# Two chained attention blocks on one core: the stacked queries of the second block loaded through ScalarE's DMA queue

## Chip, cores, metric

One Trainium2 chip, one core. The metric is the device time of one launch of the whole kernel, in microseconds (us).

## What is computed

64 independent sequences of 128 rows and 320 channels go through two blocks. Cut to what matters here:

```python
# first block (8 heads of 40): cross attention on the context, plus a small attention of four context tokens
query = x @ Wq;  keyt = enc @ Wk;  valt = enc @ Wv
hs = mha(query, keyt, valt)
x = (hs + token_attention(...)) @ Wout + b_out + x
# second block (20 heads of 16)
h1 = ln(x);  x = attn(h1, h1, q1, k1, v1, o1_w, o1_b, 20) + x     # self attention
h2 = ln(x);  x = attn(h2, context, q2, k2, v2, o2_w, o2_b, 20) + x  # cross attention
h3 = ln(x);  a, g = split(h3 @ ff_w1 + ff_b1);  x = (a * gelu(g)) @ ff_w2 + ff_b2 + x
```

The change touches the queries and keys of the second block's self attention (`h1 @ q1` and `h1 @ k1`).

## The kernel before

The 64 sequences are taken two at a time, so the loop has 32 steps and one more that drains what is still under way: it runs 33 times. The work is software-pipelined by hand. One pass of the loop holds the self attention of one pair of sequences, the first block of the next pair, and the feed-forward of an earlier one. Each engine has its own instruction stream, and within a stream all is in program order; the streams meet only at semaphores. The order is written out by hand: the table `BODY` gives the order of TensorE's outputs ("jobs"), which go round six PSUM banks, and each engine's loop lists its calls.

Scores run in units of four heads. `ALL_UNITS` numbers them: units 0 to 3 are the token attention (tile names `ca_heads`, `G`, values `VX`), 4 to 13 the self attention, 14 to 23 the cross attention (both `Qs`, `Ks`), 24 to 27 the first block (`Q0s`, `K0s`). For a unit n, `scores(i, n)` on TensorE gives the row maxima that VectorE takes, `exponents(i, n)` computes the transposed scores less the maxima, ScalarE's `exps(i, n)` writes the exponentials twice (L724 in 32 bits to `P`, L725 in 16 bits to `PT`), GpSimd's `low_probabilities(i, n)` (L501) writes the 16-bit remainder, and TensorE's `attend(i, n)` waits for that remainder (`low_p`) before it multiplies by the values.

Queries and keys are kept as a 16-bit high part and a 16-bit remainder. ScalarE writes the high part (`cQ`, `cK`, L653), VectorE the 32-bit whole, GpSimd the remainder (L508), and then they make a round trip through DRAM to be laid out by head. A **put** (`put_split`, L359) stores one of three chunks to a scratch tensor (`s_k1`, `s_q1`); a **stack** (`stack`, L363) reads a scratch tensor back by three loads of 160 KB, so that high and low parts lie in stacked partitions of `Ks` and `Qs`. All of these transfers are issued by SyncE, in the order of `one_pass` (L413 to L438). For the self attention that order is: the puts of Q0T (first-block queries), K1T and Q1T, three each; `stack_self`, which waits until all six puts of K1T and Q1T have landed (`self_put` at 96) and then issues the three loads of `Ks` and the three of `Qs`; `stack_first_queries` (three loads of `Q0s`); then the puts of K0T, the first of which waits until all six stack loads have landed (`self_stacked`).

TensorE's scores of unit 4 wait for the same six loads. `self_put` has two more readers: ScalarE's `emptied` waits for it before it overwrites `cK` (K0T) and `cQ` (Q2T).

ScalarE's stretch around the change is in its loop: three `high_shifted` of K1T, three of Q1T, `high_maxima(i, 0)` (L695), `exps(i, 0)`, `exps(i, 1)`, `high_maxima(i, 1)`, and then the first-block values and `exps(i, 2)`. It issues no DMA.

Of the kernel before, what the change touches and what calls it, by code (L numbers as in the profile page):

```python
# [14 lines left out]
D0, D1 = H // HEADS0, H // HEADS1  # L15
# [32 lines left out]
Q_PARTS = (0, 0, 1)  # L48
# [32 lines left out]
SPLITS = {"K1T": 0, "Q1T": 3, "Q2T": 6}  # L81
SPLITS_STEP = 9
LOADS_STEP = 16 * 9
STACK_LOADS, STACK_STORES = 16 * 6, 16 * 6
CROSS_STORES = 16 * 3
WAIT_BASE = 16 * 6
HEAD_LINKS, STEP_LINKS = 30, 27
# [69 lines left out]
LOOP_JOBS = Jobs(BODY)  # L157
# [24 lines left out]
def build(nc, d, out):  # L182
# [4 lines left out]
    with ctx:  # L187
# [3 lines left out]
        def sem(name):  # L191
            return ctx.enter_context(nc.semaphore(name))
# [109 lines left out]
        j_full, a_done, v_done = sem("j_full"), sem("a_done"), sem("v_done")  # L302
        low_p, pv_done, o_done = sem("low_p"), sem("pv_done"), sem("o_done")
        split_done = sem("split_done")
        self_put, q0_put, k0_put = sem("self_put"), sem("q0_put"), sem("k0_put")
        q2_put, k2_put = sem("q2_put"), sem("k2_put")
        self_stacked, first_stacked, cross_stacked = sem("self_stacked"), sem("first_stacked"), sem("cross_stacked")
        vx_ready, ca_ready = sem("vx_ready"), sem("ca_ready")
# [9 lines left out]
        def done(i, number, who):  # L318

            return (i + 1) * PER[who] + number + 1  # L320
# [26 lines left out]
        def _(sp):  # L347
# [13 lines left out]
            def stack(dst, src, e, parts, landed):  # L361
                for y, part in enumerate(parts):
                    sp.dma_start(dst[y * e:(y + 1) * e, :, :],  # L363
                                 src[part, :, :].rearrange("(h e) n -> e h n", e=e)).then_inc(landed, 16)
# [17 lines left out]

            def stack_self(i):
                sp.wait_ge(j_full, done(i - 1, LOOP_JOBS.number("T23"), "J"))
                sp.wait_ge(self_put, i * STACK_STORES + STACK_STORES)
                stack(Ks, s_k1, D1, K_PARTS, self_stacked)
                stack(Qs, s_q1, D1, Q_PARTS, self_stacked)

            def stack_first_queries(i):
                sp.wait_ge(j_full, done(i - 1, LOOP_JOBS.number("T27"), "J"))  # L390
# [23 lines left out]
            def one_pass(i, stores):  # L414
                put_low(i, "Q0T", 0, cQ, CH0, s_q0, AT0, q0_put)
                put_low(i, "Q0T", 1, cQ, CH0, s_q0, AT0, q0_put)
                put_low(i, "Q0T", 2, cQ, CH0, s_q0, AT0, q0_put)
                put_split(i, "K1T", 0, cK, s_k1, self_put)
                put_split(i, "K1T", 1, cK, s_k1, self_put)
                put_split(i, "K1T", 2, cK, s_k1, self_put)  # L420
                put_split(i, "Q1T", 0, cQ, s_q1, self_put)
                put_split(i, "Q1T", 1, cQ, s_q1, self_put)
                put_split(i, "Q1T", 2, cQ, s_q1, self_put)
                stack_self(i)
                stack_first_queries(i)
                put_low(i, "K0T", 0, cK, CH0, s_k0, AT0, k0_put, self_stacked)
                put_low(i, "K0T", 1, cK, CH0, s_k0, AT0, k0_put)
                load_next(i)
                put_low(i, "K0T", 2, cK, CH0, s_k0, AT0, k0_put)
                stack_first_keys(i)  # L430
                stack_cross_keys(i)
                put_split(i, "Q2T", 0, cQ, s_q2, q2_put, first_stacked)
                put_split(i, "Q2T", 1, cQ, s_q2, q2_put)
                put_split(i, "Q2T", 2, cQ, s_q2, q2_put)
                stack_cross_queries(i)
                put_low(i, "K2T", 0, cK, CH1, s_k2, AT1, k2_put, cross_stacked)
                put_out(i, 0, stores)
                put_out(i, 1, stores)  # L438
                put_low(i, "K2T", 1, cK, CH1, s_k2, AT1, k2_put)
                put_low(i, "K2T", 2, cK, CH1, s_k2, AT1, k2_put)  # L440
# [189 lines left out]
        def _(act):  # L630
# [9 lines left out]
            def emptied(i, name):  # L640

                return {"Q0T": (q2_put, i * CROSS_STORES + CROSS_STORES), "K1T": (k2_put, i * CROSS_STORES + CROSS_STORES),
                        "Q1T": (q0_put, i * CROSS_STORES + CROSS_STORES), "K0T": (self_put, i * STACK_STORES + STACK_STORES),
                        "Q2T": (self_put, i * STACK_STORES + STACK_STORES),
                        "K2T": (k0_put, i * CROSS_STORES + CROSS_STORES)}[name]

            def high_shifted(i, name, k, dst, c):
# [9 lines left out]
            def high_chunk(i, name, k, dst, r, f):  # L657

                bank = bank_of(i, LOOP_JOBS, f"{name}{k}")
                if k == 0:  # L660
                    act.wait_ge(factor_ready, i + 1)
                    act.wait_ge(*emptied(i, name))
                nc.scalar.activation(dst[0:r, 0, k, :], bank[0:r, 0:GS], ACT.Copy,
                                     scale=factor[0:r, f:f + 1]).then_inc(a_done, 1)

            def high_tokens(i, jobs):

# [81 lines left out]
            with nc.Fori(0, STEPS + 1, engines=[act.engine], hint_back_edge=True) as i:  # L749
                L = LOOP_JOBS  # L750
                order.restart()
                high_chunk(i, "Q0T", 0, cQ, CH0[0], FQ0)
                high_chunk(i, "Q0T", 1, cQ, CH0[1], FQ0)
                high_blocks(i, "XT0_0", hTn, 0)
                high_blocks(i, "XT0_1", hTn, 1)
                high_chunk(i, "Q0T", 2, cQ, CH0[2], FQ0)
                high_shifted(i, "K1T", 0, cK, 0)
                high_shifted(i, "K1T", 1, cK, 0)
                high_shifted(i, "K1T", 2, cK, 0)
                high_shifted(i, "Q1T", 0, cQ, 3)  # L760
                high_shifted(i, "Q1T", 1, cQ, 3)
                high_shifted(i, "Q1T", 2, cQ, 3)
                high_maxima(i, 0)
                exps(i, 0)
                exps(i, 1)
                high_maxima(i, 1)
                first_part(i, "V0", 0, V0, HEADS0, D0, factor[:, F0:F0 + 1])
                exps(i, 2)
                high_chunk(i, "K0T", 0, cK, CH0[0], FK0)
                first_part(i, "V1", 0, V1, HEADS1, D1, V1_FACTOR)  # L770
                exps(i, 3)
                high_chunk(i, "K0T", 1, cK, CH0[1], FK0)
                high_chunk(i, "K0T", 2, cK, CH0[2], FK0)
                first_part(i, "V1", 1, V1, HEADS1, D1, V1_FACTOR)
                first_part(i, "V0", 1, V0, HEADS0, D0, factor[:, F0:F0 + 1])
                high_maxima(i, 2)
                exps(i, 4)
                exps(i, 5)
                exps(i, 6)
                high_maxima(i, 3)  # L780
                exps(i, 7)
                exps(i, 8)
                exps(i, 9)
                exps(i, 10)
                exps(i, 11)
                exps(i, 12)
                exps(i, 13)
                gelu(i, L, 0)
                high_out(i, 1, 0)
                gelu(i, L, 1)  # L790
                gelu(i, L, 2)
                gelu(i, L, 3)
                high_out(i, 1, 1)
                gelu(i, L, 4)
                gelu(i, L, 5)
                high_blocks(i, "XT1_0", hTn, 0)
                high_blocks(i, "XT1_1", hTn, 1)
                high_shifted(i, "Q2T", 0, cQ, 6)
                high_shifted(i, "Q2T", 1, cQ, 6)
                high_shifted(i, "Q2T", 2, cQ, 6)  # L800
                gelu(i, L, 6)
                gelu(i, L, 7)
                gelu(i, L, 8)
                gelu(i, L, 9)
                exp4(i)
                load_exp_table()
                high_maxima(i, 4)
                high_chunk(i, "K2T", 0, cK, CH1[0], FK2)
                exps(i, 14)
                exps(i, 15)  # L810
                high_chunk(i, "K2T", 1, cK, CH1[1], FK2)
                exps(i, 16)
                high_maxima(i, 5)
                exps(i, 17)
                high_chunk(i, "K2T", 2, cK, CH1[2], FK2)
                exps(i, 18)
                exps(i, 19)
                exps(i, 20)
                exps(i, 21)
                high_maxima(i, 6)  # L820
                exps(i, 22)
                exps(i, 23)
                high_out(i, 2, 0)
                high_maxima(i, 7)
                exps(i, 24)
                exps(i, 25)
                exps(i, 26)
                exps(i, 27)
                high_out(i, 2, 1)
                first_part(i, "V2", 0, V2, HEADS1, D1, factor[:, F2:F2 + 1])  # L830
                high_out(i, 0, 0)
                first_part(i, "V2", 1, V2, HEADS1, D1, factor[:, F2:F2 + 1])
                high_out(i, 0, 1)
                high_blocks(i, "XT2_0", hT3, 0)
                high_blocks(i, "XT2_1", hT3, 1)
                high_tokens(i, L)
                assert order.next == PER["A"]
# [1072 lines left out]
```

## Time and profile before

| | us |
|---|---|
| median of 3 runs | 4137.58 |
| the three runs | 4137.58, 4140.25, 4123.45 |
| the profiled execution, device time | 4125.89 |
| its span, first to last instruction | 4124.0 |
| TensorE busy in it | 3767.4 (91%) |
| ScalarE busy in it | 2225.3 (54%) |
| VectorE, GpSimd busy in it | 2501.0 (61%), 1981.5 (48%) |

The profile is of one execution; the device time lies 1.9 us over its span. In its lists a wait stands with the group of instructions that waited and with what ended the wait; "L363" is a line of the kernel; names of tiles stand as written<-read, and buffer numbers are left out. DMA issues stand on the queue of the engine that issues them (SPq is SyncE's), with the time that the issue took; the landing is told apart. PEclk is the granted clock of TensorE as a share of full speed, 1.00 at 2.4 GHz and 0.50 at 1.2 GHz.

### The profile page before, as it was taken

Reading aid. Unit: us, or ns where it says so; the run is one execution under the profiler, and the core shown is the slowest. Engines: PE = TensorE matmul, PEld = TensorE weight load, DVE = VectorE, ACT = ScalarE, POOL = GpSimd, SP = SyncE. Lnnn points to the kernel's source line nnn. Section 1 sums busy time; section 2 is a strip of 40 time slices with the busy share of each in tenths; the row PEclk is TensorE's granted clock in tenths of the full one; section 3 lists DMA queues with packets and bytes.
Section 4 is the critical chain, followed back from the end, with each engine's and each line's share of the span. In section 5 each row is a group of like instructions: output and inputs, shape, how many; then the busy total and the mean of one; then the engine's idle time right before and its main releaser. Section 6 shows DMA issues by size and latency. Waiting matters only on the chain.

```text
span 4124.0 us, 114798 instructions
## 1 busy us (share of the span) xinstructions
PE 3767.4 (91%) x39220; PEld 3033.2 (74%) x39220; DVE 2501.0 (61%) x6482; ACT 2225.3 (54%) x3834; POOL 1981.5 (48%) x2297
## 2 busy tenths in 40 slices
PE   4899999999999999999999999999999999999999
PEld 4677777777777777777777777777777777777777
DVE  7565655566566556656655565665556566555655
ACT  1465555545545554655555455555555555555554
POOL 0445454544544554454455445445445544554453
PEclk9899999999999998999999899999989999998999
DMA  4323222333322333332233323223332322333230
GB/s 137 57 55 58 47 46 49 62 59 57 62 42 46 55 61 60 57 62 42 47 54 58 62 56 63 43 47 54 59 62 56 61 45 49 52 58 62 56 64 19
DMA packets 393942, 230.78 MB, mean 56 GB/s; under 512 B 24807, under 2 KB 393055, under 8 KB 393183
## 3 DMA queue, kind: packets, MB, share of 16 engines
q1 hardware_dynamic: 393566, 224.70, 28.9%
q8 instruction: 366, 6.00, 0.7%
q14 instruction: 10, 0.07, 0.0%
HBM read 148.59 MB, written 76.02 MB: 54 GB/s over the span
## 4 chain that ended last, share of the span: by engine, by line
issue 42%; POOL 41%; PE 11%; DVE 4%; POOLq 2%; ACT 0%; DMA 0%; DVEq 0%; SPq 0%; ACTq 0%
POOL PT L501 24%; PE bank L1377 11%; POOL ca_heads L542 3%; POOL rstd L550 2%; POOL XB L478 2%; POOL cK L508 2%; POOL cQ L508 2%; POOL VX L526 1%; POOL OA L525 1%; POOL XA L478 1%; POOL rstd L549 1%; POOL X L478 1%; POOLq L500 1%; POOL ca L541 1%; POOL ca L539 0%
## 5 line engine op out<-in xcount | busy, mean ns | idle before, releaser
L501 POOL TENSOR_TENSOR PT<-P,PT 128x512 f16<-128x512 f32 (+1 forms) x924 | 1069.2, 1157 | 778.3 <-ACT PT L725 778.3
L976 DVE TENSOR_REDUCE mx<-bank 128x4 f32<-128x512 f32 (+1 forms) x924 | 582.7, 680 | 107.9 <-PE bank L1377 103.9
L1377 PE MATMUL bank<-hT,w_ff_w 128*128 128x256 f16 x5440 | 644.4, 273 | 1.7 <-DVE hT L1005 1.5
L1377 PEld LDWEIGHTS bank<-hT,w_ff_w 128*128 128x128 f16 x5440 | 523.3, 98 | 74.8 <-issue 7.9
L1377 PE MATMUL bank<-mxs,pick 84*128 84x128 f16 (+1 forms) x3696 | 543.7, 229 | 0.0
L1377 PEld LDWEIGHTS bank<-mxs,pick 84*128 84x128 f16 (+1 forms) x3696 | 394.2, 109 | 25.9 <-issue 14.5
L1377 PE MATMUL bank<-Qs,Ks 96*128 96x128 f16 x2640 | 382.3, 228 | 27.4 <-DVE mxs L985 27.0
L1377 PE MATMUL bank<-w_ff,F 128*128 128x320 f32 x1360 | 401.5, 438 | 1.3 <-DVE F L1052 1.3
L706 ACT ACTIVATE P<-bank,ff_b,scale 128x256 f32<-128x256 f32 x340 | 192.0, 565 | 370.2 <-PE bank L1377 271.4
L1377 PEld LDWEIGHTS bank<-V,PT 128*128 128x128 f16 (+1 forms) x9504 | 313.6, 96 | 76.4 <-POOL PT L501 51.3
L1377 PE MATMUL bank<-V,PT 128*128 128x17 f16 (+1 forms) x9504 | 346.5, 173 | 17.2 <-POOL PT L501 12.6
L1023 DVE RECIPROCAL rden<-bank 128x20 f32<-128x20 f32 (+1 forms) x264 | 64.0, 242 | 481.5 <-PE bank L1377 480.5
L1377 PEld LDWEIGHTS bank<-w_ff,F 128*128 128x128 f32 x1360 | 245.3, 190 | 83.2 <-DVE F L1052 1.5
L1377 PEld LDWEIGHTS bank<-Qs,Ks 96*128 96x128 f16 x2640 | 266.2, 102 | 54.5 <-DVE mxs L985 34.5
L724 ACT ACTIVATE P<-bank,log_p,exp_self 128x512 f32<-128x512 f32 x330 | 255.2, 773 | 76.9 <-PE bank L1377 76.7
L724 ACT ACTIVATE P<-bank,log_p,out_factor 128x512 f32<-128x512 f32 x330 | 254.6, 771 | 75.5 <-PE bank L1377 68.4
L508 POOL TENSOR_TENSOR cQ<-whole,cQ 128x256 f16<-128x256 f32 (+1 forms) x198 | 132.2, 668 | 312.1 <-DVE whole L869 312.1
L869 DVE TENSOR_SCALAR whole<-bank,factor,qk_b 128x256 f32<-128x256 f32 (+1 forms) x297 | 160.8, 541 | 186.9 <-ACT cQ L653 156.0
L549 POOL TENSOR_TENSOR rstd<-mv,eps 128x1 f32<-128x1 f32 x198 | 41.5, 209 | 455.3 <-DVE mv L1040 455.3
L724 ACT ACTIVATE P<-bank,log_p,factor 124x512 f32<-124x512 f32 (+1 forms) x264 | 205.2, 777 | 100.8 <-PE bank L1377 97.6
L725 ACT ACTIVATE PT<-bank,log_p,out_factor 128x512 f16<-128x512 f32 x330 | 253.3, 768 | 0.0
L725 ACT ACTIVATE PT<-bank,log_p,exp_self 128x512 f16<-128x512 f32 x330 | 253.3, 768 | 0.0
(282 smaller groups left out, 7814.3 us busy)
## 6 DMA issues: line engine op xcount, KB each, us to landing
Ks<-scratch_k SPq DMA_DIRECT2D x198, 160.0 KB, 5.4
Qs<-scratch_q SPq DMA_DIRECT2D x198, 160.0 KB, 5.7
scratch_k<-cK SPq DMA_DIRECT2D x134, 128.0 KB, 1.8
scratch_q<-cQ SPq DMA_DIRECT2D x134, 128.0 KB, 1.8
Q0s<-scratch_q SPq DMA_DIRECT2D x99, 160.0 KB
K0s<-scratch_k SPq DMA_DIRECT2D x99, 160.0 KB
cT<-in_cT SPq DMA_DIRECT2D x136, 96.0 KB, 2.0
xin<-in_x SPq DMA_DIRECT2D x34, 320.0 KB, 3.2
```

The costliest lines, as they stand in the source:

```text
L478: nc.gpsimd.tensor_tensor(dst[:, b, :], src[:, b, :], bias[:, j, :], ALU.add).then_inc(ready, 1)
L501: nc.gpsimd.tensor_tensor(PT[0:keys, n % PT_SLOTS, 1, :], P[0:keys, n % P_SLOTS, :], PT[0:keys, n % PT_SLOTS, 0, :], ALU.subtract).then_in ...
L508: nc.gpsimd.tensor_tensor(dst[0:r, 1, k, :], whole[0:r, m % 3, :], dst[0:r, 0, k, :], ALU.subtract)\
L542: nc.gpsimd.tensor_tensor(ca_heads[:, :, :], ca16[:, :].unsqueeze(1).to_broadcast([rows, HEADS0, GS]), mask_ca[:, :].unsqueeze(2).to_broad ...
L549: link(i, nc.gpsimd.tensor_tensor(rstd[:, j, b:b + 1], mv[:, j, b, 1:2], eps[:, :], ALU.add))
L550: nc.gpsimd.tensor_tensor(rstd[:, j, b:b + 1], rstd[:, j, b:b + 1], minus_half[:, :], ALU.pow)\
L706: nc.scalar.activation(gate[:, t % 2, :], bank[:, 0:GS], ACT.Gelu, scale=scale[:, 1:2], bias=ff_b[:, FFT + t:FFT + t + 1]).then_inc(a_done, 1)
L724: nc.scalar.activation(P[0:keys, n % P_SLOTS, :], bank[0:keys, :], ACT.Exp, bias=log_p[0:keys, :], scale=by)
L725: nc.scalar.activation(PT[0:keys, n % PT_SLOTS, 0, :], bank[0:keys, :], ACT.Exp, bias=log_p[0:keys, :], scale=by).then_inc(a_done, 1)
L869: nc.vector.tensor_scalar(whole[0:r, m % 3, :], bank[0:r, 0:GS], factor[0:r, FQ2:FQ2 + 1], qk_b[0:r, c + k:c + k + 1], ALU.mult, ALU.add). ...
L976: nc.vector.tensor_reduce(mx[:, g % 2, 4 * u:4 * u + 4], bank[:, :].rearrange("p (h s) -> p h s", h=4)[:, :, 0:keys], axis=AX.X, op=ALU.ma ...
L1377: return nc.tensor.matmul(o, lhsT, rhs, start=start, stop=stop)
```

## The change

`self_put`, one semaphore for six puts, becomes `k1_put` and `q1_put`, 48 each. `stack_self` on SyncE waits for the three puts of K1T alone and issues only the three loads of `Ks`. A new `stack_queries` on ScalarE, called between `high_maxima(i, 0)` and `exps(i, 0)`, waits for the three puts of Q1T and issues the three loads of `Qs` from ScalarE's own DMA queue. `emptied` reads `k1_put` for K0T and `q1_put` for Q2T. All six loads still count on `self_stacked`, whose readers are unchanged. Nothing else moves in any stream.

```diff
@@ SyncE
             def stack_self(i):
                 sp.wait_ge(j_full, done(i - 1, LOOP_JOBS.number("T23"), "J"))
-                sp.wait_ge(self_put, i * STACK_STORES + STACK_STORES)
+                sp.wait_ge(k1_put, i * CROSS_STORES + CROSS_STORES)
                 stack(Ks, s_k1, D1, K_PARTS, self_stacked)
-                stack(Qs, s_q1, D1, Q_PARTS, self_stacked)
...
-                put_split(i, "K1T", 0, cK, s_k1, self_put)
+                put_split(i, "K1T", 0, cK, s_k1, k1_put)
...
-                put_split(i, "Q1T", 0, cQ, s_q1, self_put)
+                put_split(i, "Q1T", 0, cQ, s_q1, q1_put)
...
@@ ScalarE
-                        "Q1T": (q0_put, i * CROSS_STORES + CROSS_STORES), "K0T": (self_put, i * STACK_STORES + STACK_STORES),
-                        "Q2T": (self_put, i * STACK_STORES + STACK_STORES),
+                        "Q1T": (q0_put, i * CROSS_STORES + CROSS_STORES), "K0T": (k1_put, i * CROSS_STORES + CROSS_STORES),
+                        "Q2T": (q1_put, i * CROSS_STORES + CROSS_STORES),
...
+            def stack_queries(i):
+
+                act.wait_ge(j_full, done(i - 1, LOOP_JOBS.number("T23"), "J"))
+                act.wait_ge(q1_put, i * CROSS_STORES + CROSS_STORES)
+                for y, part in enumerate(Q_PARTS):
+                    nc.scalar.dma_start(Qs[y * D1:(y + 1) * D1, :, :],
+                                        s_q1[part, :, :].rearrange("(h e) n -> e h n", e=D1)).then_inc(self_stacked, 16)
...
                 high_maxima(i, 0)
+                stack_queries(i)
                 exps(i, 0)
```

## Rows read from the trace of the kernel before

**Rows 1.** The page, part 1 (engines) and part 2 (granted TensorE clock by slice)

```profile
PE 3767.4 (91%) x39220; PEld 3033.2 (74%) x39220; DVE 2501.0 (61%) x6482; ACT 2225.3 (54%) x3834; POOL 1981.5 (48%) x2297
...
PEclk9899999999999998999999899999989999998999
```

**Rows 2.** Waits of TensorE: us in total, times, longest

```profile
PE bank L1377 <- DVE mxs L985: 88.3, 73, 1.9
...
PE bank L1377 <- POOL PT L501: 34.3, 60, 1.0
...
PE bank L1377 <- DMA Qs<-scratch_q: 9.6, 18, 0.8
```

**Rows 3.** TensorE's groups: forms, xcount, busy us, mean ns, idle before by releaser

```profile
L1377 PE MATMUL bank<-Ks,Qs 96*128 96x128 f16 x2640 | 204.1, 227 | 13.8 <-DMA Qs<-scratch_q 9.6 <-ACT PT L725 4.2
...
L1377 PE MATMUL bank<-VX,PT 128*128 128x41 f16 x1584 | 63.5, 184 | 21.7 <-POOL PT L501 21.7
```

**Rows 4.** Whole steps, one window each: length, busy, PEclk, DMA share, GB/s

```profile
128.90:252.90 124.00, 116.11 (x1176) 93.23 (x1176) 72.80 (x191) 66.84 (x116) 59.67 (x70) 0.90 0.27 51
...
3864.70:3981.50 116.80, 107.64 (x1176) 86.85 (x1176) 72.90 (x192) 66.51 (x115) 59.66 (x70) 0.99 0.29 56
...
sum 3852.60, PE 3573.01 PEld 2871.18 DVE 2335.75 ACT 2133.09 POOL 1909.22; mean PE 111.66 PEld 89.72 DVE 72.99 ACT 66.66 POOL 59.66
```

**Rows 5.** 12 us of each step, from 4 us behind the first maxima copy

```profile
132.90:144.90 12.00, 12.00 (x77) 8.17 (x76) 2.85 (x8) 6.39 (x12) 8.36 (x9) 0.63 1.04 129
...
256.90:268.90 12.00, 10.45 (x114) 8.18 (x114) 5.92 (x19) 7.06 (x14) 9.45 (x10) 1.00 1.03 125
```

**Rows 6.** Timeline of one step, SyncE's queue: start, us, tiles, xcount

```profile
2178.11 2.43 SPq L359 DMA_DIRECT2D scratch_q<-cQ  x3
2182.05 1.33 SPq L363 DMA_DIRECT2D Ks<-scratch_k  x3
2183.43 1.46 SPq L363 DMA_DIRECT2D Qs<-scratch_q  x3
2185.07 2.31 SPq L363 DMA_DIRECT2D Q0s<-scratch_q  x3
```

**Rows 7.** The same stretch, ScalarE

```profile
2178.43 0.25 ACT L695 ACTIVATE mxs<-bank 8x128 f16<-8x128 f32 x1
...
2181.28 0.78 ACT L724 ACTIVATE P<-bank,log_p,factor 128x512 f32<-128x512 f32 x1 [2.60 <-PE bank L1377]
...
2183.95 0.25 ACT L695 ACTIVATE mxs<-bank 8x128 f16<-8x128 f32 x1
```

**Rows 8.** The same stretch, GpSimd

```profile
2182.81 1.16 POOL L501 TENSOR_TENSOR PT<-P,PT 128x512 f16<-128x512 f32 x1 [2.88 <-ACT PT L725]
```

**Rows 9.** The same stretch, TensorE: attend of the first unit, second-block scores

```profile
2184.02 0.47 PE L1377 MATMUL bank<-VX,PT 128*128 128x41 f16 x12 [1.04 <-POOL PT L501]
...
2193.48 1.06 PE L1377 MATMUL bank<-Ks,Qs 96*128 96x128 f16 x16 [0.55 <-DMA Qs<-scratch_q]
```

**Rows 10.** The step before it: SyncE, ScalarE, GpSimd, TensorE

```profile
2061.74 1.33 SPq L363 DMA_DIRECT2D Ks<-scratch_k  x3
...
2061.36 0.78 ACT L724 ACTIVATE P<-bank,log_p,factor 128x512 f32<-128x512 f32 x1 [3.00 <-PE bank L1377]
...
2062.88 1.16 POOL L501 TENSOR_TENSOR PT<-P,PT 128x512 f16<-128x512 f32 x1 [3.27 <-ACT PT L725]
...
2064.44 0.63 PE L1377 MATMUL bank<-VX,PT 128*128 128x41 f16 x12
```

**Rows 11.** Tile Qs: durations min/median/max of its loads' issues, and issue to landing

```profile
L363 SPq DMA_DIRECT2D Qs<-scratch_q x198: 326/457/468, 133.7 to 4042.9; - x198
...
DMA to landing us min/median/max: 3.3/5.7/9.4
```

**Rows 12.** Waits of SyncE's queue

```profile
SPq L363 <- DMA scratch_q<-cQ: 86.9, 64, 1.5
```

More of the change, by code:

```diff
@@ L83 @@
 LOADS_STEP = 16 * 9
-STACK_LOADS, STACK_STORES = 16 * 6, 16 * 6
+STACK_LOADS = 16 * 6
 CROSS_STORES = 16 * 3
@@ L304, in build @@
         split_done = sem("split_done")
-        self_put, q0_put, k0_put = sem("self_put"), sem("q0_put"), sem("k0_put")
+        k1_put, q1_put, q0_put, k0_put = sem("k1_put"), sem("q1_put"), sem("q0_put"), sem("k0_put")
         q2_put, k2_put = sem("q2_put"), sem("k2_put")
@@ L417, in one_pass @@
                 put_low(i, "Q0T", 2, cQ, CH0, s_q0, AT0, q0_put)
-                put_split(i, "K1T", 0, cK, s_k1, self_put)
-                put_split(i, "K1T", 1, cK, s_k1, self_put)
-                put_split(i, "K1T", 2, cK, s_k1, self_put)
-                put_split(i, "Q1T", 0, cQ, s_q1, self_put)
-                put_split(i, "Q1T", 1, cQ, s_q1, self_put)
-                put_split(i, "Q1T", 2, cQ, s_q1, self_put)
+                put_split(i, "K1T", 0, cK, s_k1, k1_put)
+                put_split(i, "K1T", 1, cK, s_k1, k1_put)
+                put_split(i, "K1T", 2, cK, s_k1, k1_put)
+                put_split(i, "Q1T", 0, cQ, s_q1, q1_put)
+                put_split(i, "Q1T", 1, cQ, s_q1, q1_put)
+                put_split(i, "Q1T", 2, cQ, s_q1, q1_put)
                 stack_self(i)
```

## Prediction

> **What bounds the kernel now.** I began with the page's engine table. TensorE is busy 91% of the span and the next engine 61% [rows 1], so a delay counts if it reaches TensorE, and a gain counts if TensorE was waiting. The second view is therefore TensorE's list of waits. The loads that the change touches stand in it with 9.6 us in 18 waits, 0.53 us each [rows 2], and the groups show that all of them are in front of the scores of `Qs` and `Ks` [rows 3]. No other DMA that the loop issues stands among TensorE's waits, so 9.6 us of 4126 is all that earlier stacks can give directly. The same list has 34.3 us of waits for the low probabilities `PT` of GpSimd [rows 2], of which 21.7 us in 22 waits are in front of `attend` on `VX`, the token attention [rows 3]. That wait lies just behind the place where ScalarE gets its new work.
>
> The third view is the step as a whole. There are 32 windows from one step to the next, 120.4 us on average (3852.60 / 32). They fall into two kinds: 16 with the granted clock at 0.97 or above, on average 117.8 us, and 16 at 0.90 to 0.94, on average 123.0 us [rows 4] (an early slow one, the last, a quick one, and the sum). TensorE's clock thus makes 5.1 us of difference in a step. In the 12 us behind the place of the change, 18 of 33 windows have a clock of 1.00 and 15 have 0.53 to 0.67 [rows 5] (the first of each kind); 18 is also the number of waits for `Qs`. So in the quick steps TensorE is early and waits half a microsecond for `Qs`; in the slow ones it runs at half clock and `Qs` is there before it.
>
> **The change part by part.** I take one quick step and the slow step before it.
>
> *What ScalarE now does ahead of the exponentials.* It waits for the last put of Q1T to land. In the quick step that is when SyncE now issues the first load of `Ks`, at 2182.05 [rows 6]; it is held by that landing, since SyncE's queue waits at this line for a put of queries, up to 1.5 us [rows 12]. Then ScalarE issues three loads. On SyncE the same three took 1.46 us [rows 6], one 326 to 468 ns [rows 11]. Nothing in the trace shows what an issue costs ScalarE. The bounds are 0 (only the wait is left) and 2.31 us, which three `Q0s` loads took on SyncE with loads queued ahead of them [rows 6]. I take 1.46, because these are the same transfers. The Trainium skill ("Perfetto Trace Analysis", DMA Instruction — HWDGE) says that the issuing sequencer is occupied until the descriptors are generated and only then takes its next instruction; no row here shows it for ScalarE, and by it the value is the same 1.46.
>
> *What is queued behind it.* `exps(0)`, `exps(1)`, `high_maxima(1)`, then the values. `exps(0)` started at 2181.28 [rows 7] and would start at 2182.05 + 1.46 = 2183.5, 2.2 us later (0.8 to 3.1 by the bounds). GpSimd starts the low part 1.53 us behind that (2182.81 [rows 8]), and TensorE's `attend` starts as soon as it is done: at 2184.02, already after 1.04 us of waiting [rows 9]. There is no slack, so `attend` comes 2.2 us later and that wait grows to 3.3 us. `high_maxima(1)` moves from 2183.95 [rows 7] to about 2186.2; the `T2` product that needs it comes after the first-block values and is covered.
>
> *What it costs in a quick step.* From `attend` to the scores of `Qs` TensorE has one stretch of work that ended at 2193.48 − 0.55 = 2192.9, and then it waited 0.55 us for `Qs` [rows 9]. With 2.2 us more ahead of it, it gets there at 2195.2. The 0.5 us of waiting is gone, covered by the new delay, and 1.7 us are left. 18 × 1.7 = 31 us.
>
> *In a slow step.* The put landed at 2061.74 and `exps(0)` had started at 2061.36, so it is delayed by 0.38 + 1.46 = 1.8 us. The low part then ends at 2062.88 + 1.16 + 1.84 = 2065.9, and `attend`, which went at 2064.44 without a wait [rows 10], is late by 1.4. 15 × 1.4 = 21 us.
>
> *The loads.* `Ks` is issued when the last put of Q1T has been issued, 2178.11 + 2.43 = 2180.5, instead of 2182.05; `Qs` at 2182.05 instead of 2183.43; but `Q0s`, which stood behind `Qs`, now goes out at about 2181.9 [rows 6] and shares the engines with it. At worst `Qs` is the last of nine loads of 160 KB: 1475 kB at 125 GB/s, as in the 12 us of a quick step [rows 5], is 11.8 us from 2181, so about 2193. TensorE comes at 2195.2, or at 2193.7 if issuing costs ScalarE nothing. So I cost the new order of loads at nothing; if that cover is gone, it costs the lateness at one for one. The put of K0T, which waits for the six loads, and the first-block stacks can be late without anybody waiting: no wait of TensorE names them [rows 2]. `emptied` now reads earlier counts, and ScalarE comes there later than both: nothing.
>
> *The sum of the waits alone:* 31 + 21 = 52 us.
>
> *The clock.* TensorE's longest wait in the loop is now 1.9 us, in front of `exponents` for the maxima `mxs` [rows 2], and 1.04 us at `attend` come a little behind. With these two, the clock was low near here in 15 of 33 steps. The second now becomes 3.3 us, longer than any wait of the loop. What share of the 18 quick steps then falls to half clock no row tells: between none and all. I take 11, two in three, at the 5.1 us between the two kinds: 11 × 5.1 = 56 us. Bounds 0 and 18 × 5.1 = 92.
>
> Together 52 + 56 = 108 us. Against the profiled execution's 4125.9 that is 4234; the median of the runs is 12 us above that execution, and the three differ by 17, so I take half of it: 4240.
>
> **The rivals.**
> - *Held, but the clock stays as it is.* For it: the waits that precede a fall are there in both kinds of step. Then 4126 + 52 + 6 = 4184.
> - *Issuing costs ScalarE next to nothing.* Only the wait for the put remains: 0.77 us in a quick step, of which the 0.55 at the scores gives back most (18 × 0.22 = 4), and 0.38 in a slow one, up to 15 × 0.4 = 6. 4136, with half the median's offset 4142. For it: a DMA issue isn't counted as busy. The Trainium skill ("DMA: Bandwidth & Descriptors", Issuing engines are not separate DMA queues) calls the saved issue time usually small and says that all issuers share the 16 DMA engines; the share of 1.03 in [rows 5] agrees that these engines are full here, so a second queue brings `Qs` no sooner than bytes allow.
> - *ScalarE is held longer*, because SyncE issues `Q0s` in the same microseconds: 2.31 us for three and the wait, 3.1 in a quick step less 0.5, 2.7 − 0.4 in a slow one: 18 × 2.6 + 15 × 2.3 = 81, and all 18 steps lose their clock, 92: 4126 + 81 + 92 + 6 = 4305.
> - *Faster.* TensorE's 9.6 us for `Qs` goes, because `Ks` starts 1.5 us and `Qs` 1.4 us earlier, and `attend` isn't delayed: 4126 − 10 + 6 = 4122. It needs ScalarE to get past the put before 2181.28. Against it: the put lands at 2182.05 and nothing ahead of it has changed [rows 6, 7].
>
> **How the numbers follow.** Chances: forecast (around 4240) 0.50, held with an unchanged clock 0.20, issue nearly free 0.12, held longer 0.13, faster 0.05. Range 4145 to 4310: it takes in the forecast with 0 to 18 falls and the second bound of the issue, and leaves out the case of a free issue and the faster one. A measurement of this kernel can tell about 0.5% from no change, that is 4117 to 4158: faster 0.05, same 0.12, slower 0.83.
>
> **What the profile after would show.** On ScalarE's queue three loads of `Qs`, each taking some 0.3 to 0.5 us, and `exps(0)` behind the last of them, about 5 us behind the end of the first maxima copy instead of 2.6 to 3.0. TensorE's wait for `PT` at `attend` on `VX` grows from 21.7 us to 18 × 3.3 + 15 × 1.4 = 80 us. The wait for `Qs` at the scores is gone. More than 15 of 33 windows behind that place have a clock under 1.00. The forecast is wrong if ScalarE's issue is far from 0.5 us, if `attend` turns out to have slack, or if the loads land later than 2195 on this scale, so that the wait for `Qs` grows instead.

## The result, and the profile after

The changed kernel takes 4293.6 us (median of four runs, 4293.0 to 4294.0) against 4138.8 for the kernel before (one run more than ahead of the prediction): a ratio of 1.038, 95% interval 1.036 to 1.041. It is slower, by 155 us; the forecast was 4240 with a range of 4145 to 4310. The profiled execution has a span of 4291.5 us, 167.5 more than the one before.

The page of the changed kernel: engines, granted clock by slice, and ScalarE's new DMA queue (q10).

```profile
PE 3851.2 (90%) x39220; PEld 3108.6 (72%) x39220; DVE 2494.4 (58%) x6482; ACT 2223.6 (52%) x3834; POOL 1979.2 (46%) x2297
...
PEclk9999999999999998999999999999999999999999
...
q10 hardware_dynamic: 33264, 16.23, 3.8%
```

Against [rows 1]: the same 39220 matmuls take 3851.2 us instead of 3767.4. So TensorE is busy 83.8 us longer with the same work, which is a lower clock (0.927 granted on average, 0.947 before); the other 83.7 of the 167.5 are idle time. VectorE, ScalarE and GpSimd are busy no longer than before. Where the idle time is, TensorE's waits of the changed kernel tell (us in total, times, longest), and its groups (busy us, mean ns, idle before by releaser):

```profile
PE bank L1385 <- POOL PT L500: 126.0, 68, 3.5
PE bank L1385 <- DVE mxs L993: 85.0, 72, 1.9
```

```profile
L1385 PE MATMUL bank<-Ks,Qs 96*128 96x128 f16 x2640 | 226.5, 242 | 0.5 <-DMA Qs<-scratch_q 0.5
L1385 PE MATMUL bank<-VX,PT 128*128 128x41 f16 x1584 | 62.8, 183 | 113.6 <-POOL PT L500 113.6
```

[Rows 2, 3] had 34.3 us of waits for `PT`, 21.7 of them in front of `attend` on `VX`; now it is 126.0 and 113.6. The wait for `Qs` at the scores of `Ks` fell from 9.6 us to 0.5, and the idle time of that group from 13.8 to 0.5. So the one group gained 13.3 us and the other lost 91.9.

Whole steps of the changed kernel, as in [rows 4]: two neighbours and the sum of the 32.

```profile
2387.40:2513.50 126.10, 114.99 (x1176) 92.56 (x1176) 72.86 (x192) 66.63 (x116) 59.61 (x70) 0.92 0.30 52
2513.50:2637.20 123.70, 112.06 (x1176) 90.06 (x1176) 72.96 (x192) 66.64 (x116) 59.62 (x70) 0.94 0.30 53
...
sum 4013.60, PE 3652.47 PEld 2943.72 DVE 2329.26 ACT 2131.43 POOL 1906.82; mean PE 114.14 PEld 91.99 DVE 72.79 ACT 66.61 POOL 59.59
```

A step takes 125.4 us (4013.60 / 32) instead of 120.4. The quick steps, with a clock of 0.99 and 107.6 us of busy TensorE [rows 4], are gone. The 12 us behind the place of the change show why (as in [rows 5]; 32 of the 33 windows have 0.72 as the second line, one has 0.59):

```profile
1638.30:1650.30 12.00, 9.03 (x52) 6.03 (x52) 2.37 (x6) 6.47 (x11) 7.54 (x8) 0.59 1.04 108
...
2391.40:2403.40 12.00, 8.55 (x49) 5.77 (x49) 2.28 (x6) 6.00 (x11) 7.53 (x8) 0.72 1.02 108
```

No window is at 1.00 any more, where 18 of 33 were. One step in the timeline (start, us, tiles, number; in brackets the idle time before and what ended it), where the first maxima copy ends at 2135.54:

```profile
2135.29 0.25 ACT L702 ACTIVATE mxs<-bank 8x128 f16<-8x128 f32 x1
2137.61 1.44 SPq L363 DMA_DIRECT2D Ks<-scratch_k  x3
2138.95 1.33 ACTq L670 DMA_DIRECT2D Qs<-scratch_q  x3
2139.23 1.16 SPq L363 DMA_DIRECT2D Q0s<-scratch_q  x3
2140.55 0.78 ACT L731 ACTIVATE P<-bank,log_p,factor 128x512 f32<-128x512 f32 x1 [5.01 <-PE bank L1526]
2142.07 1.15 POOL L500 TENSOR_TENSOR PT<-P,PT 128x512 f16<-128x512 f32 x1 [5.29 <-ACT PT L732]
2143.28 0.60 PE L1385 MATMUL bank<-VX,PT 128*128 128x41 f16 x12 [3.45 <-POOL PT L500]
2143.72 2.48 PE L1385 MATMUL bank<-w_Wv,cT 96*128 96x320 f32 x4
...
2155.17 1.06 PE L1385 MATMUL bank<-Ks,Qs 96*128 96x128 f16 x16
```

Read it from the top. The loads of `Qs` are issued from 2138.95 to 2140.28, and `exps(0)`, which stands behind them in ScalarE's stream, starts at 2140.55, 5.01 us behind the maxima copy (2.60 and 3.00 in [rows 7, 10]). The label "<-PE bank" on its idle time misleads: for that bank alone it would have started at 2.60 as in [rows 7]; the profile counts neither the semaphore wait nor the three issues as work. GpSimd follows 1.52 us later, TensorE waits 3.45 us, and the product behind the wait, four matmuls on `cT`, takes 2.48 us. In the quick step of [rows 9], at full clock, it took 1.32:

```profile
2184.33 1.32 PE L1377 MATMUL bank<-w_Wv,cT 96*128 96x320 f32 x4
```

So at the end of that wait the clock drops to half. The scores of `Ks` start 19.6 us behind the maxima copy; in [rows 9] it was 14.8.

### The profile page after: what moved, and what is told of

Its sections match the earlier page's. It is cut to its first block, busy times and chain, and to the rows that moved or that the text cites. A ratio compares the mean times of both kernels' runs of the same rounds, so it can differ in the third digit from the quotient of the medians.

```text
span 4291.5 us, 114831 instructions
## 1 busy us (share of the span) xinstructions
PE 3851.2 (90%) x39220; PEld 3108.6 (72%) x39220; DVE 2494.4 (58%) x6482; ACT 2223.6 (52%) x3834; POOL 1979.2 (46%) x2297
## 4 chain that ended last, share of the span: by engine, by line
issue 43%; POOL 40%; PE 11%; DVE 4%; POOLq 1%; ACT 0%; DMA 0%; DVEq 0%; SPq 0%; ACTq 0%
POOL PT L500 23%; PE bank L1385 10%; POOL ca_heads L541 3%; POOL rstd L549 2%; POOL XB L477 2%; POOL cK L507 2%; POOL cQ L507 2%; POOL XA L477 1%; POOL VX L525 1%; POOL OA L524 1%; POOL rstd L548 1%; POOL X L477 1%; POOLq L499 1%; POOL ca L540 1%; POOL ca L538 0%
## 5 line engine op out<-in xcount | busy, mean ns | idle before, releaser
L1385 PE MATMUL bank<-mxs,pick 84*128 84x128 f16 (+1 forms) x3696 | 562.0, 234 | 0.0
L1385 PEld LDWEIGHTS bank<-mxs,pick 84*128 84x128 f16 (+1 forms) x3696 | 405.5, 112 | 31.7 <-issue 18.3
L1385 PE MATMUL bank<-Qs,Ks 96*128 96x128 f16 x2640 | 401.0, 235 | 24.1 <-DVE mxs L993 23.7
L1385 PEld LDWEIGHTS bank<-Qs,Ks 96*128 96x128 f16 x2640 | 276.4, 106 | 50.2 <-DVE mxs L993 31.2
L1385 PE MATMUL bank<-hTn,w_q 128*128 128x256 f16 (+1 forms) x1584 | 256.9, 331 | 0.0
```

Of the source, the lines that this page charges most:

```text
L1385: return nc.tensor.matmul(o, lhsT, rhs, start=start, stop=stop)
```

## The experiments

Each is timed beside the kernel before on the same chip. The median of that kernel was 4138.8 us beside the changed kernel, 4127.6 beside e1 to e4, 4118.3 beside e5 to e8 and 4116.6 beside e9 to e11, so kernels of different groups are best compared by ratio. "Held" stands for the theory of the forecast: three issues and their wait hold ScalarE, hence `attend`, hence TensorE's clock. The base is told with each; line numbers differ a little between kernels.

**e1: keys early alone** (base: the kernel before). The split semaphores and the early `Ks`, with `Qs` still on SyncE behind a wait of its own; ScalarE issues nothing.

```diff
-                sp.wait_ge(self_put, i * STACK_STORES + STACK_STORES)
+                sp.wait_ge(k1_put, i * CROSS_STORES + CROSS_STORES)
                 stack(Ks, s_k1, D1, K_PARTS, self_stacked)
-                stack(Qs, s_q1, D1, Q_PARTS, self_stacked)
...
+            def stack_self_queries(i):
+                sp.wait_ge(q1_put, i * CROSS_STORES + CROSS_STORES)
+                stack(Qs, s_q1, D1, Q_PARTS, self_stacked)
...
                 stack_self(i)
+                stack_self_queries(i)
```

> The change without its ScalarE part: the semaphores are split and the keys' loads go out as soon as the keys are put, but the queries' loads stay on SyncE's queue, behind a wait for their own puts; ScalarE issues nothing. Theory 'ScalarE is held' (the wait for the puts and the three issues on ScalarE delay the first exponentials, TensorE waits for their low part, and the clock falls behind that wait): back to the time of before, 4110 to 4150, first exponentials 2.6 to 3.0 us behind the first maxima copy, wait for PT in front of attend on VX about 22 us in all, wait for Qs at the scores below the 9.6 us of before, because the loads start 1.4 us earlier. Rival 'loads' (what costs is that keys' loads now go out while the puts land, or that first-block loads share the engines with the queries'): the part of it that the early keys cause stays, 4200 or more.

Measured: 4111.4 us, ratio 0.995 (0.993 to 0.997). `Qs` lands 12.7 us behind the maxima copy (median; 14.6 before), the scores no longer wait for it, and `attend` waits as before:

```profile
L1389 PE MATMUL bank<-Ks,Qs 96*128 96x128 f16 x2640 | 202.7, 226 | 4.8 <-ACT PT L737 4.3
L1389 PE MATMUL bank<-VX,PT 128*128 128x41 f16 x1584 | 63.0, 183 | 26.3 <-POOL PT L505 26.3
```

The half of the change that concerns the keys is a small gain by itself (0.5%), so the loss is in the other half.

**e2: the wait without the issues** (base: e1). ScalarE waits for the puts of Q1T ahead of `exps(0)`, and issues nothing.

```diff
                 high_maxima(i, 0)
+                act.wait_ge(q1_put, i * CROSS_STORES + CROSS_STORES)
                 exps(i, 0)
```

> As e1_keys_early, but ScalarE waits for the queries' puts ahead of the first exponentials, and issues nothing. It parts the wait from the three issues. Theory 'ScalarE is held': first exponentials at 3.4 to 3.5 us behind the first maxima copy (2.6 to 3.0 before, 5.0 after the change), the wait at attend about 1.9 us in a quick step, so 18 x 0.3 + 15 x 0.4 = 11 us of waits, and the clock falls in some more of the 33 steps than the 15 of before: 4140 to 4220. Rival 'the issues are what holds' (the wait is hidden): 4110 to 4150. Rival 'the wait is all': 4280 to 4300.

Measured: 4183.6 us, ratio 1.013 (1.008 to 1.017). In one step:

```profile
1359.88 0.78 ACT L736 ACTIVATE P<-bank,log_p,factor 128x512 f32<-128x512 f32 x1 [3.70 <-DMA scratch_q<-cQ]
...
1362.62 0.47 PE L1390 MATMUL bank<-VX,PT 128*128 128x41 f16 x12 [2.14 <-POOL PT L505]
```

The exponentials start at 3.70, `attend` waits 2.14 us, and the clock falls just behind it in 32 of 33 steps (in e1 and in the kernel before in none). The waits at `attend` come to 70.0 us, 44 more than in e1, where 11 more were expected: all steps but one wait the 2.14 us, those that had been slow too. From e1 to the changed kernel the ratio goes from 0.995 to 1.038, some 180 us; 0.017 of it (72 us) is the wait for the put alone, and the other 0.026 comes with the issues.

**e9: one issue of three** (base: the changed kernel). SyncE issues the first two loads of `Qs`, ScalarE only the third.

```diff
+            def stack_self_queries(i):
+                sp.wait_ge(q1_put, i * CROSS_STORES + CROSS_STORES)
+                stack(Qs, s_q1, D1, Q_PARTS[0:2], self_stacked)
...
+                stack_self_queries(i)
...
                 act.wait_ge(q1_put, i * CROSS_STORES + CROSS_STORES)
-                for y, part in enumerate(Q_PARTS):
+                for y, part in ((2, Q_PARTS[2]),):
```

> Keys early as in the changed kernel, but ScalarE issues only the third load of the queries, ahead of the first exponentials; SyncE issues the other two behind its own wait for the puts of Q1T. ScalarE is held: one issue less than the changed kernel's three leaves about 0.3 to 0.5 us on ScalarE, so the exponentials start about 4.0 us behind the first maxima copy (3.7 with the wait alone, 5.0 with three issues), attend waits about 2.4 us in every step, the clock falls in all 33 steps, and the time is 4190 to 4240, nearer the kernel with the wait alone (4184). Rival, what counts is that a second queue carries query loads at all: near the changed kernel's 4290. Rival, issues cost nothing: 4184, with attend's wait at 2.1.

Measured: 4204.4 us, ratio 1.021 (1.018 to 1.024). One step, with the issue at 309 ns:

```profile
1351.21 0.31 ACTq L675 DMA_DIRECT2D Qs<-scratch_q  x1
...
1351.79 0.78 ACT L736 ACTIVATE P<-bank,log_p,factor 128x512 f32<-128x512 f32 x1 [4.01 <-DMA scratch_q<-cQ]
...
1354.53 0.47 PE L1390 MATMUL bank<-VX,PT 128*128 128x41 f16 x12 [2.44 <-POOL PT L505]
```

Zero, one and three issues give starts of 3.70, 4.01 and 5.02, waits of 2.14, 2.44 and 3.45, and 4184, 4204 and 4294 us (ratios 1.013, 1.021 and 1.038). What ScalarE issues appears one for one at `attend`.

**e8: the landing sooner in the changed kernel** (base: the changed kernel). SyncE holds the first-block stacks back until `Ks` and `Qs` have landed.

```diff
             def stack_first_queries(i):
+                sp.wait_ge(self_stacked, i * STACK_LOADS + STACK_LOADS)
```

> The changed kernel with the same one edit as e7_behind_alone: first-block loads only behind the six self loads. Theory 'ScalarE is held': the queries land sooner than 15.5 us, at 12.5 to 14, and nothing comes of it, because TensorE reaches the scores at 19.8 us: 4280 to 4300, wait at attend on VX about 114 us. Rival 'loads' (the later landing is part of the cost): 4260 or less.

Measured: 4294.0 us, ratio 1.042 (1.039 to 1.045), the time of the changed kernel. `Qs` lands 3.1 us sooner (12.7 instead of 15.8) and nothing is gained:

```profile
L1386 PE MATMUL bank<-Ks,Qs 96*128 96x128 f16 x2640 | 226.1, 242 | 0.0
L1386 PE MATMUL bank<-VX,PT 128*128 128x41 f16 x1584 | 62.7, 183 | 113.1 <-POOL PT L501 113.1
```

The order of the loads costs nothing in the changed kernel, as the forecast had it: `attend` comes too late for it to matter.

**e3 and e7: ScalarE issues later.** e3 is the changed kernel with the three issues behind `high_maxima(1)`; e7 is e3 with e8's wait on SyncE.

```diff
                 high_maxima(i, 0)
-                stack_queries(i)
                 exps(i, 0)
                 exps(i, 1)
                 high_maxima(i, 1)
+                stack_queries(i)
```

> The change with the same three loads on ScalarE's queue, but called behind the first two exponentials and the second maxima copy. Theory 'ScalarE is held': first exponentials again 2.6 to 3.0 us behind the first maxima copy, the wait for PT at attend on VX back at about 22 us; the queries are issued at about 5.6 instead of 3.4 us and land 1 to 2 us later than after the change, so the scores wait for Qs 1 to 3 us in the quick steps, 20 to 50 us in all: 4140 to 4200. Rival 'loads' (a second queue beside SyncE's is what costs): stays at 4270 to 4310.

> e3_loads_behind, where the queries' loads on ScalarE's queue were issued at 4.5 us and landed only at 18 to 19 us, with one edit: SyncE waits for the six self loads before it issues the three first-block loads. Theory 'sharing' (the queries on the second queue are late because the first-block loads run beside them): the queries land at 13 to 14.7 us, the scores wait at most 0.6 us, 4105 to 4150. Rival 'the second queue is slow by itself': they land at 16 us or later, 4200 or more.

Measured: e3 4257.4 us, ratio 1.030 (1.023 to 1.036); e7 4097.8, ratio 0.995 (0.992 to 0.997). The first lines are e3's, the second e7's:

```profile
L1385 PE MATMUL bank<-Ks,Qs 96*128 96x128 f16 x2640 | 238.5, 250 | 100.0 <-DMA Qs<-scratch_q 97.0 <-DVE V L898 2.2 <-ACT PT L732 0.8
L1385 PE MATMUL bank<-VX,PT 128*128 128x41 f16 x1584 | 69.9, 192 | 24.8 <-POOL PT L500 24.8
```

```profile
L1386 PE MATMUL bank<-Ks,Qs 96*128 96x128 f16 x2640 | 200.2, 225 | 5.3 <-ACT PT L733 5.2
L1386 PE MATMUL bank<-VX,PT 128*128 128x41 f16 x1584 | 62.6, 183 | 29.6 <-POOL PT L501 29.6
```

In both, `attend` has its old wait back. But e3 turned the loss into another one, larger than the 20 to 50 us expected: issued on ScalarE about a microsecond later, with `Q0s` already on its way from SyncE, `Qs` lands at 18.6 us and the scores wait for it, 97.0 us in all. In e7, without `Q0s` beside it, it lands at 12.8 and the loss is gone. The cover that the forecast named for the landing is thus real: it was ScalarE's own delay.

**e6 and e10: a longer cover at `attend`** (base: e1). TensorE computes the first part of the first-block values ahead of `attend(0)` instead of behind it; e10 adds e8's wait.

```diff
+                values(i, "V0", 0, "Wv", cT)
                 attend(i, 0)
-                values(i, "V0", 0, "Wv", cT)
```

> e1_keys_early (no load on ScalarE's queue) with V0_0 called ahead of the first attend: the reverse of the change, 1.3 us of real work take the place of the 1.04 us in which TensorE waits for the low part there. If the wait and the clock behind it are what counts at this place: the wait at attend on VX falls from 26 us to under 5, fewer than 12 of 33 steps have a low clock there, and the time falls from 4111 to 4050 to 4095. Rival 'the wait only moves' (to the product for T2, which needs the second maxima): 4105 to 4120.

> The first-block values ahead of the first attend, keys early, queries on SyncE, and the first-block stacks not issued before the second block's six loads have landed. ScalarE is held predicts that attend waits for nothing, as in the kernel with the values ahead, and that the queries land about 12.5 us behind the first maxima copy instead of 13.2 to 13.5, so the small wait at the scores goes: 4070 to 4085. Rival, the landing is covered either way: 4083, no difference. Rival, the first-block stacks now come late for their own scores: above 4090, with a wait for Q0s in TensorE's list.

Measured: e6 4082.7 us, ratio 0.990 (0.987 to 0.993); e10 4088.4, ratio 0.992 (0.990 to 0.995), not told apart from e6. e6's groups:

```profile
L1389 PE MATMUL bank<-Ks,Qs 96*128 96x128 f16 x2640 | 223.9, 240 | 7.0 <-DMA Qs<-scratch_q 5.8 <-ACT PT L737 0.8
L1389 PE MATMUL bank<-VX,PT 128*128 128x41 f16 x1584 | 61.4, 181 | 0.0
```

`attend` never waits, and only one step in 33 is at half clock near it; but in 29 steps the clock then falls 18 us behind the maxima copy, and its time at the low level is 432 us in all, nearly as before (436). Of the 34.1 us by which the span is shorter than before, 3.3 are busy time, so nearly all of the gain is idle time. e6 is the fastest of the study: 1.0% under the kernel before, with ScalarE issuing nothing.

**e11: the same cover in the changed kernel.**

> The changed kernel with the first-block values on TensorE ahead of the first attend, which gives TensorE work while ScalarE issues. ScalarE is held: attend's wait shrinks from 3.45 us by the length of that work, about 1.3, to 2.1; the clock still falls in all 33 steps as it did with a wait of 2.14. The time is 4294 less 33 x 1.3 = 43, about 4250 (4235 to 4260). If the clock stays high in many steps it goes to 4150 to 4200. Rival, the delay of ScalarE costs elsewhere than at attend (the values' own copies, the second exponentials): no gain, 4285 to 4300.

Measured: 4193.2 us, ratio 1.017 (1.014 to 1.020). Its span, 4195.1 us, is 96.4 under the changed kernel's, where 43 were expected.

```profile
PE 3788.9 (90%) x39220; PEld 3062.1 (73%) x39220; DVE 2488.8 (59%) x6482; ACT 2220.0 (53%) x3834; POOL 1978.2 (47%) x2297
...
L1385 PE MATMUL bank<-VX,PT 128*128 128x41 f16 x1584 | 62.9, 183 | 69.4 <-POOL PT L500 69.4
```

The wait at `attend` shrinks by 44.2 us (113.6 to 69.4), as expected. What was missed is that TensorE's busy time shrinks too, by 62.3 us: the clock still falls in most steps (28 just behind `attend`), but its time at the low level goes from 626 to 503 us. The exponentials start as late as in the changed kernel, at 5.02, and yet the span is within 2.4 us of that of e2, where they start at 3.71 and the waits at `attend` are alike (70.0 us). So the delay of ScalarE costs what it makes TensorE wait; no cost elsewhere shows.

**e4 and e5: dummy products ahead of `attend`.** They were to keep TensorE busy through the wait and so to part the clock from the wait. e4 puts 26 16-bit products ahead of `attend(0)` in the changed kernel, e5 the values and 8 32-bit ones.

```diff
+                fill(i, "V0_0", 26)
                 attend(i, 0)
```

> The changed kernel with 26 products of 128x256 that nobody reads on TensorE ahead of the first attend, in a bank that the next real product overwrites: they take the place of the 3.45 us in which TensorE stood still there. It parts the clock from the wait. Theory 'held, and the clock falls behind the wait': attend starts when it did, about 7.8 us behind the first maxima copy, but the clock stays at 1.00 in more than half of the steps, and the time falls to 4170 to 4230. Rival 'the clock falls for another reason' or 'the wait itself is the whole cost': 4280 to 4320.

> The changed kernel, with TensorE's first-block value product (V0_0, 1.3 us) called ahead of the first attend, and behind it 8 products of 120x256 in 32 bits that nobody reads, in the bank of the next job: together about as long as the 3.45 us in which TensorE stood still there, with few added instructions. It parts the clock from the wait once more. Theory 'held, and the clock falls behind the wait': attend still at about 7.8 us, the clock stays at 1.00 there in most steps, scores start at 15.5 to 16.5 us instead of 19.8: 4120 to 4190. Rival 'the clock falls for another reason': only the value product's 33 x 1.3 us comes back, 4240 to 4260.

Measured: e4 4275.7 us, ratio 1.035 (1.030 to 1.040); e5 4346.6, ratio 1.054 (1.051 to 1.057). Neither could part the two. The loads of `Qs` on ScalarE in e4 and in e5 (ns min/median/max):

```profile
L670 ACTq DMA_DIRECT2D Qs<-scratch_q x99: 309/482/1945, 132.4 to 4106.8; - x99
```

```profile
L670 ACTq DMA_DIRECT2D Qs<-scratch_q x99: 309/482/2167, 132.6 to 4211.1; - x99
```

In every step one of the three issues, nearly always the third, took 1.7 to 2.2 us instead of 0.48, so that the exponentials started at 6.3 and the wait to be filled was itself longer. In e5 the clock had fallen ahead of the dummies, which then ran at half clock and past the end of the wait. In e4 it was better than in the changed kernel: 459 us at the low level against 626, with a fall ahead of `attend` in 20 steps, just behind it in 4 and neither in 9. But the dummies are busy time themselves, 3869.2 us of TensorE in all against 3851.2. So filling the wait with useless work kept the clock up in some steps of e4, and that it pays is not shown; that shortening the wait with useful work pays is (e6, e11).

**Side by side.** Start of `exps(0)` and landing of `Qs` are medians behind the end of the first maxima copy; the wait is the idle time in front of the `VX` group; "falls" are steps of 33 in which the clock falls at the end of that wait or just behind it.

| kernel | us | ratio | `exps(0)` | wait at `attend` | `Qs` landed | falls | TensorE busy |
|---|---|---|---|---|---|---|---|
| e6 | 4082.7 | 0.990 | 2.60 | 0 | 13.4 | 0 | 3764.1 |
| e7 | 4097.8 | 0.995 | 2.61 | 29.6 | 12.8 | 0 | 3735.0 |
| e1 | 4111.4 | 0.995 | 2.60 | 26.3 | 12.7 | 0 | 3756.6 |
| before | 4138.8 | 1 | 2.60 | 21.7 | 14.6 | 0 | 3767.4 |
| e2 | 4183.6 | 1.013 | 3.71 | 70.0 | 12.8 | 32 | 3790.3 |
| e11 | 4193.2 | 1.017 | 5.02 | 69.4 | 15.7 | 28 | 3788.9 |
| e9 | 4204.4 | 1.021 | 4.00 | 80.5 | 13.0 | 33 | 3782.4 |
| after | 4293.6 | 1.038 | 5.02 | 113.6 | 15.8 | 32 | 3851.2 |
| e8 | 4294.0 | 1.042 | 5.02 | 113.1 | 12.7 | 32 | 3849.4 |

e2 and e11 wait alike at `attend`, one because of the put alone, the other because of three issues with a cover in front, and they have nearly the same time and the same busy TensorE. Above the 30 us of the first four, the time follows that wait, whatever makes it: from e1 to e2 the span grows by 76.6 us for 43.7 us of wait (4116.1 to 4192.7), from e2 to after by 98.8 for 43.6 (to 4291.5). A microsecond of wait here costs 1.8 to 2.3 by the spans, 1.7 to 2.5 by the medians (72 and 110 us, the second across groups): one that is idle, and about one more in clock (33.7 and 60.9 us of busy time). How rough that is shows e9, which has 10.5 us more wait than e2 for 4.3 us more span, or 21 by the medians.

## Why the prediction was right, point by point

- *ScalarE's new work.* Taken at 1.46 us for three issues, measured 1.33, 309 to 489 ns each; the first issue came 3.42 us behind the maxima copy, 3.37 was worked out. `exps(0)` was put at 4.8 and started at 5.02. The Trainium skill ("Perfetto Trace Analysis", DMA Instruction — HWDGE) has the issuing sequencer occupied until the descriptors are made; the timeline agrees, with `exps(0)` 0.27 us behind the end of the third issue.
- *What is queued behind it.* 3.3 us of wait at `attend` in a quick step, measured 3.45. No slack, as said. The other things behind `exps(0)` show no cost (e11 beside e2).
- *The loads.* Costed at nothing, and nothing it was (e8); the wait for `Qs` at the scores went, as said. But the landing was put too early, at 2193 at worst, which is 14.3 us behind the maxima copy; it came at 15.8. The 16.5 (2195.2) worked out for the scores would have covered it by 0.7 us; they came at 19.6, most of that by the lower clock.
- *The slow steps: mis-sized.* The forecast let them lose 1.4 us each, 21 in all, on the grounds that TensorE came to `attend` late, at half clock. In the changed kernel the clock in these steps no longer falls ahead of `attend` (1 step of 33, where it was 15) but behind it (32). So TensorE is there on time in every step and waits the whole 3.45 (2.97 in one step). All 33 together are 113.6 us, where the forecast's check was 80. The 15 slow steps therefore lose about 15 × 2 = 31 us more than was said, of which part comes back as higher clock ahead of `attend`.
- *The clock: right in kind, too few falls.* 11 of 18 quick steps were to fall; all 18 did. That share was a guess between bounds, and the seven falls that it missed are 36 us at its own 5.1. The rows show what a step pays: 107.64 us of busy TensorE in a quick step [rows 4], 112.06 or 114.99 now; 116.11 in a slow one, which hence gains a little. Averaged over all 32 windows of that view, it was 108.6 in a quick step, 114.7 in a slow one, and is 114.1 now: a fall costs 5.5 us, near the 5.1 that was taken. In sum +83.8 us where 56 were said and 92 was the bound.
- *The sum.* 52 for waits and 56 for the clock were forecast, against 83.7 of idle time and 83.8 of busy time. That both pairs are nearly equal is in part luck: the 5.1 us was a difference of step lengths, in which more busy time (6.1 us) is offset by shorter waits. In the forecast's own terms, nearly all of the 59.5 us missing from the 167.5 are the seven falls (36) and the waits of the slow steps (31), less some 9 that the slow steps gain in busy time. By kind of step, with [rows 4]: the quick steps went from 117.8 to 125.4, 7.6 longer where 1.7 and 3.1 were said on average, and the slow ones from 123.0, 2.4 longer where 1.4 were said.
- *The rivals.* "Clock unchanged" (4184) falls by the busy time. "Issue nearly free" (4142) falls by e2, e9 and the changed kernel, 4184, 4204 and 4294. "Held longer" (4305) is the nearest in time, but for another reason: its price of 2.31 us for the issues did not come, only its 18 falls of 18 and a wait in every step. "Faster" (4122) needed ScalarE to pass the put in time; e1 shows that the keys' part alone would have given it.
- *A rule that sounds harmless.* The Trainium skill ("DMA: Bandwidth & Descriptors", Issuing engines are not separate DMA queues) calls the sequencer time that a second issuer saves usually small relative to the DMA itself. Here the 1.33 us was not saved but moved from SyncE, which has slack, to ScalarE, which at this place has none; with the wait in front of it, it is worth some 4%, the step from e1 (ratio 0.995) to the changed kernel (1.038).

## What to carry to other kernels

A DMA issued by a compute engine is an instruction in that engine's stream, with the wait that it needs, and the profile counts neither as busy: cost it as work ahead of the next instruction, and look who waits for that one. Where the bound engine waits at that place already, every microsecond is idle time there, and here it brought nearly as much again in clock. The cheap halves were the others: splitting the semaphore so that the keys go early, and moving independent work of the bound engine in front of the wait, together 1.0% faster without a second queue.

## What had not been expected of the hardware

- The clock's falls moved with the wait: 15 falls ahead of `attend` and none behind it became 1 and 32. With a wait of about 1.04 us at `attend` no fall came just behind it (before, e1, e7); with 2.14 us and more it came in 28 to 33 steps of 33. e6, without a wait there, had a fall later in the step and nearly as much time at the low level (432 us, 436 before): there, removing the wait moved the fall and did not remove it.
- The same three transfers landed at 15.8 us when `Q0s` was issued beside them from another queue, and at 12.7 when it was held back (after, e8); at 18.6 and 12.8 when they were issued a microsecond later (e3, e7). With all of them on SyncE's queue, `Q0s` last, it was 12.7 (e1). What order on one queue had given them, two queues took away.
- An issue can take 1.7 to 2.2 us instead of 0.48 (one in each step of e4 and e5). A packet of the instruction queue starts within 0.6 us of the start of each of these 66 issues, and near none of the 99 in the changed kernel. But short issues of e4 and e5 have such packets near them too, and the third load of `Q0s` on SyncE took 1.4 to 2.2 us in all 33 steps of the kernel before, with no such packet near, and 0.40 in the changed kernel. The cause stays open.
